# Last forward transform of a four-layer spectral kernel: three result copies moved to VectorE, row products split into row halves

## What is computed

```
def _L3_conv_ref(x, weights):
    x_f = jnp.fft.rfft2(x)
    k_f = jnp.fft.rfft2(weights)
    out_f = jnp.einsum('bchw,ochw->bohw', x_f, k_f)
    return jnp.fft.irfft2(out_f, s=(H, W))
...
x = x + _L0_conv_ref(_gn(x), L0_conv_weights_r, L0_conv_weights_i)
x = x + _L1_conv_ref(_gn(x), L1_conv_gain)
x = x + _L2_conv_ref(_gn(x), L2_conv_weight)
x = x + _L3_conv_ref(_gn(x), L3_conv_weights)
```

## Time and profile before

| | before |
|---|---|
| runs (us) | 966.1, 970.06, 970.32; median 970.06 |
| profiled execution (us) | 970.67 |
| its span (us) | 968.9 |
| busy over the span | TensorE 782.8 (81%), VectorE 599.5 (62%), ScalarE 517.0 (53%), GpSimd 122.5 (13%) |
| granted TensorE clock over the span | 0.928 |
| granted TensorE clock in the last forward stage | 1.00 |
| last forward stage, four groups | 668.70 to 763.17 us of the span |

### The profile page before, as it was taken

The page is one execution under the profiler, slowest core; times in us unless marked ns, Lnnn a source line. Parts: engine busy times, 40 slices in busy tenths (PEclk is TensorE's granted clock), DMA queues, the critical chain, the costliest instruction groups (busy, mean ns, idle before and its releaser), DMA issues. The chain is left out here.

```text
span 968.9 us, 27289 instructions
## 1 busy us (share of the span) xinstructions
PE 782.8 (81%) x10775; PEld 654.1 (68%) x10775; DVE 599.5 (62%) x1112; ACT 517.0 (53%) x868; POOL 122.5 (13%) x120
## 2 busy tenths in 40 slices
PE   5999996853599665787599999984888588879998
PEld 5999995743588543666444444444777488879997
DVE  2555446655856689588777777776666677742222
ACT  0133246743443273465379999004887657765564
POOL 0000000100010044265301222100000100001110
PEclk9999998987789989699799999997999789999999
DMA  7499968532000010000000000004000448831222
GB/s 278 181 342 362 315 206 215 126 87 74 4 1 0 15 26 0 1 1 0 0 2 1 1 1 1 1 1 104 2 0 0 87 88 175 179 81 40 101 107 100
DMA packets 44553, 80.08 MB, mean 83 GB/s; under 512 B 19130, under 2 KB 37568, under 8 KB 40656
## 3 DMA queue, kind: packets, MB, share of 16 engines
q1 hardware_dynamic: 27856, 62.48, 22.7%
q10 hardware_dynamic: 16640, 16.78, 5.1%
HBM read 50.74 MB, written 27.92 MB: 81 GB/s over the span
## 5 line engine op out<-in xcount | busy, mean ns | idle before, releaser
L1462 DVE SCALAR_TENSOR_TENSOR X<-bank,c_power,X 32x512 f32 x128 | 96.8, 756 | 36.5 <-PE bank L1412 32.9
L914 DVE TENSOR_TENSOR X<-X,bank 128x512 f32 x64 | 43.6, 682 | 92.1 <-PE bank L900 92.1
L1605 PE MATMUL bank<-m_xp,m_kf 128*32 128x64 f32 x2048 | 81.7, 246 | 21.7 <-DVE m_xp L1540 10.1
L1605 PEld LDWEIGHTS bank<-m_xp,m_kf 128*32 128x32 f32 x2048 | 80.7, 172 | 22.9 <-issue 22.8
L429 ACT COPY ks_spec<-bank 128x512 f32<-128x512 f32 x64 | 34.3, 589 | 98.6 <-PE bank L357 98.6
L411 DVE COPY ks_rows<-bank 128x512 f32<-128x512 f32 x64 | 41.2, 687 | 70.9 <-PE bank L342 70.9
L215 DVE BATCH_NORM_STATS2 bn<-X 128x6 f32 x128 | 83.1, 683 | 2.9 <-POOL X L1202 1.6
L342 PE MATMUL bank<-ks_fw,ks_src 64*128 64x64 f32 x1024 | 68.7, 298 | 11.2 <-DMA ks_src<-in_L_conv_weights 11.2
L1368 ACT ACTIVATE c_r<-X,c_nrm 32x1024 f32 (+1 forms) x56 | 75.1, 1341 | 2.5 <-DVE c_nrm L1436 1.1
L342 PEld LDWEIGHTS bank<-ks_fw,ks_src 64*128 64x128 f32 x1024 | 68.1, 215 | 11.2 <-issue 11.2
L357 PE MATMUL bank<-ks_fh,ks_rows 64*128 64x128 f32 (+1 forms) x1152 | 71.2, 277 | 0.1
(11 more groups left out here) (186 smaller groups left out, 1869.2 us busy)
## 6 DMA issues: line engine op xcount, KB each, us to landing
ks_src<-in_L_conv_weights SPq DMA_DIRECT2D x8, 2048.0 KB, 8.2
kf<-ks_spec ACTq DMA_DIRECT2D x16, 1024.0 KB, 9.3
m_kf<-kf SPq DMA_DIRECT2D x32, 512.0 KB, 8.5
X<-in_x SPq DMA_DIRECT2D x4, 2048.0 KB, 13.8
out_y<-X SPq DMA_DIRECT2D x16, 512.0 KB, 2.6
xf<-f_xm SPq DMA_DIRECT2D x6, 448.0 KB
l_wb<-in_L_conv_weights_r SPq DMA_DIRECT2D x4, 512.0 KB, 11.0
l_wb<-in_L_conv_weights_i SPq DMA_DIRECT2D x4, 512.0 KB, 13.3
```

The source lines that it names most:

```text
L914: dve.tensor_tensor(x, x, ps[4 + c % 4][:], ALU.add).then_inc(added, 1)
L1462: dve.scalar_tensor_tensor(x, of.rearrange("p (y x) -> p y x", x=HN), filt.power[at, 2:3], x, ALU.mult, ALU.add).then_inc(added, 1)
L1605: last = pe.matmul(ps[4 * half + m // 8][at:at + C, m % 8 * N:(m % 8 + 1) * N], kf[p][:, j, :, H * half + m], xp[half][:, j, m].rearrange( ...
```

## The change

`Forward` gets two more arguments. L0's stage passes `halves` as False and keeps its order. L3's passes True, other tables of normalisation, and `kept_by_dve` = (1, 3, 5).

```
-    def __init__(self, pr, ctx, name, mats, slot_at, rows_by_act, norm_by_act, norm_by_dve):
-        self.pr, self.slot_at = pr, slot_at
+    def __init__(self, pr, ctx, name, mats, slot_at, rows_by_act, norm_by_act, norm_by_dve, halves, kept_by_dve=()):
+        self.pr, self.slot_at, self.halves = pr, slot_at, halves
+        self.keeper = [0 if s in kept_by_dve else 1 for s in range(len(slot_at))]
...
+        self.kept = [pr.sem(f"{name}_kept{e}") for e in range(2)]
...
+    def wait_kept(self, pe, q, first, to):
+        for e in range(2):
+            if e in self.keeper[first:to]:
+                pe.wait_ge(self.kept[e], START + self.keeper.count(e) * q + self.keeper[:to].count(e))
...
+            def half_products(q, j):
+                if j in (0, 2):
+                    self.wait_kept(pe, q - 1, S - 4 + j, S - 2 + j)
+                elif j % 2 == 0:
+                    self.wait_rows(pe, q, j - 3)
+                for k in range(4):
+                    at, col = slice(k * P, (k + 1) * P), (j % 2 * 4 + k) * N
+                    for t, (part, mat) in enumerate(((self.th, 0), (self.th, 1), (self.tl, 0))):
+                        for a in range(2):
+                            half = slice(a * N, (a + 1) * N)
+                            m = pe.matmul(ps[4 + j // 2 % 2 * 2 + a][:, col:col + N], part[j % 4][half, at],
+                                          self.fw[half, mat, half], start=t == 0, stop=t == 2)
+                return m
...
                 pe.wait_ge(self.turned_read, G * q + j + 1)
+                if self.halves:
+                    m = half_products(q, j)
+                    m.then_inc(self.made, 1)
+                    continue
...
     def copy_rows(self, eng, copy, q, j):
+        if self.halves:
+            eng.wait_ge(self.made, self.G * q + j // 2 * 2 + 2)
+            first = j // 2 * 2 * ROWS
+            copy(self.rows[:, first + j % 2:first + 2 * ROWS:2].rearrange("p h r k -> p h (r k)"),
+                 self.pr.psum[4 + j // 2 % 2 * 2 + j % 2][:].rearrange("p (h n) -> p h n", h=ROWS)
+                 ).then_inc(self.rows_read[self.by[j]], 1)
+            return
...
             def keep_filling(s):
-                act.wait_ge(self.made, G * q + NCH + s + 1)
-                keep(q, s).then_inc(self.kept, 1)
+                if self.keeper[s]:
+                    act.wait_ge(self.made, G * q + NCH + s + 1)
+                    keep(q, s).then_inc(self.kept[1], 1)
...
+            def keep_filling(s):
+                if not self.keeper[s]:
+                    dve.wait_ge(self.made, G * q + NCH + s + 1)
+                    keep(q, s).then_inc(self.kept[0], 1)
...
-                if j and not self.by[j - 1]:
-                    self.copy_rows(dve, dve.tensor_copy, q, j - 1)
...
+                behind = 2 if self.halves else 1
+                if j >= behind and not self.by[j - behind]:
+                    self.copy_rows(dve, dve.tensor_copy, q, j - behind)
...
                 normalise_next(NCH + s)
+                if s >= 3:
+                    keep_filling(s - 3)
+            for s in range(S - 3, S):
+                keep_filling(s)
...
-        fwd = Forward(pr, ctx, "f3", mats, SLOT_AT, True, {2: 0, 4: 1, 6: 2, 8: 3}, {9: 4, 10: 5, 12: 6, 14: 7})
+        fwd = Forward(pr, ctx, "f3", mats, SLOT_AT, True, {2: 0, 4: 1}, {3: 2, 8: 3, 9: 4, 11: 5, 13: 6, 14: 7}, True, (1, 3, 5))
```

More of the change, by code:

```diff
@@ L457, in __init__ @@
         self.fw, self.fh, self.fh0 = mats
-        self.turned, self.turned_read, self.high, self.made, self.kept = (
-            pr.sem(f"{name}_{n}") for n in ("turned", "turned_read", "high", "made", "kept"))
+        self.turned, self.turned_read, self.high, self.made = (
+            pr.sem(f"{name}_{n}") for n in ("turned", "turned_read", "high", "made"))
+        self.kept = [pr.sem(f"{name}_kept{e}") for e in range(2)]
         self.ready = [pr.sem(f"{name}_ready{c}") for c in range(NCH)]
@@ L505, in products @@
                 pe.wait_ge(self.turned_read, G * q + j + 1)
+                if self.halves:
+                    m = half_products(q, j)
+                    m.then_inc(self.made, 1)
+                    continue
                 if j < 4:
-                    pe.wait_ge(self.kept, START + S * q + j - 3)
+                    self.wait_kept(pe, q - 1, S - 4 + j, S - 3 + j)
                 else:
@@ L532, in products @@
                 if s >= 4:
-                    pe.wait_ge(self.kept, START + S * q + s - 3)
+                    self.wait_kept(pe, q, s - 4, s - 3)
                 width = self.fh.shape[-1]
@@ L553, in high_parts @@
         pr, ps, S, G = self.pr, self.pr.psum, self.S, self.G
-        act.sem_inc(self.kept, START)
+        for e in range(2):
+            act.sem_inc(self.kept[e], START)
         def group(q, more):
@@ L593, in high_parts, with low_parts @@
         group(Q - 1, False)
-    def low_parts(self, dve):
+    def low_parts(self, dve, keep=None):
         pr, ps, S, G = self.pr, self.pr.psum, self.S, self.G
@@ L614, in group @@
                 normalise_next(j)
-                if j and not self.by[j - 1]:
-                    self.copy_rows(dve, dve.tensor_copy, q, j - 1)
-            if not self.by[NCH - 1]:
-                self.copy_rows(dve, dve.tensor_copy, q, NCH - 1)
+                behind = 2 if self.halves else 1
+                if j >= behind and not self.by[j - behind]:
+                    self.copy_rows(dve, dve.tensor_copy, q, j - behind)
+            for j in range(NCH - behind, NCH):
+                if not self.by[j]:
+                    self.copy_rows(dve, dve.tensor_copy, q, j)
             for s in range(S):
@@ L647, in l0_forward_stage @@
         fwd = Forward(pr, ctx, "f0", mats, [[S * k + s for k in range(4)] for s in range(S)],
-                      False, {1: 0, 3: 1, 5: 2, 7: 3, 9: 4, 11: 5}, {8: 6, 10: 7})
+                      False, {1: 0, 3: 1, 5: 2, 7: 3, 9: 4, 11: 5}, {8: 6, 10: 7}, False)
         xm = pr.sb(ctx, "f0_xm", [P, 2, S, KX, 2, IB])
@@ L715, in _ @@
                     for s in range(S):
-                        pool.wait_ge(fwd.kept, START + S * q + s + 1)
+                        pool.wait_ge(fwd.kept[1], START + S * q + s + 1)
                         pool.tensor_tensor(xm[:, 1, s, :, 0, :], pr.zero[:].unsqueeze(2).broadcast_to([P, KX, IB]),
@@ L1473, in l3_forward_stage, with keep @@
     with ExitStack() as ctx:
-        fwd = Forward(pr, ctx, "f3", mats, SLOT_AT, True, {2: 0, 4: 1, 6: 2, 8: 3}, {9: 4, 10: 5, 12: 6, 14: 7})
+        fwd = Forward(pr, ctx, "f3", mats, SLOT_AT, True, {2: 0, 4: 1}, {3: 2, 8: 3, 9: 4, 11: 5, 13: 6, 14: 7}, True, (1, 3, 5))
+        def keep(copy, q, s):
+            return copy(xm[:, s, :, :, bass.ds(IB * q, IB)].rearrange("p k r b -> p b r k"),
+                        pr.psum[4 + s % 4][:].rearrange("p (b r k) -> p b r k", b=IB, r=2))
         with pr.nc.Block() as block:
@@ L1486, in _ @@
             def _(dve):
-                fwd.low_parts(dve)
+                fwd.low_parts(dve, lambda q, s: keep(dve.tensor_copy, q, s))
             @block.scalar
             def _(act):
-                fwd.high_parts(act, lambda q, s: act.copy(
-                    xm[:, s, :, :, bass.ds(IB * q, IB)].rearrange("p k r b -> p b r k"),
-                    pr.psum[4 + s % 4][:].rearrange("p (b r k) -> p b r k", b=IB, r=2)))
+                fwd.high_parts(act, lambda q, s: keep(act.copy, q, s))
 def load_kernel_spectra(sp, pr, to, i, pair, loaded):
```

## The result

| | before | after |
|---|---|---|
| median of 20 runs (us) | 970.77 (966.1 to 977.34) | 974.78 (969.6 to 977.23) |
| profiled execution, its span (us) | 970.67, 968.9 | 972.49, 970.7 |
| last forward stage in the span | 668.70 to 763.17: 94.47 us | 666.88 to 761.90: 95.02 us |
| mixing, first product to the next stage's first cast of results | 776.68 to 872.43: 95.75 us | 775.40 to 874.22: 98.82 us |
| granted clock over the span | 0.928 | 0.912 |

The ratio of after to before is 1.0032, 95% interval [1.0016, 1.0048]: **slower by 0.32%**, some 3.1 us (the two medians lie 4.0 apart), where 2.6 less was forecast. In the two profiles the forward stage is 0.55 us longer and the mixing 3.07, together 3.6. What lies between them takes 13.5 us in both, what lies behind 96.5.

The account below looks back on a forecast made before the run. An order of waits, not one engine, bounds the last forward stage's groups. Row phases 4 x 0.2, column phases 3 x 0.23 + 1.08: 2.6 us less than 970.06, 967.5 us; range 961.5 to 976.

Parts of the forecast that it names:

- Half products: Row products of 64 rows by 64 columns: one every 0.017 us, 0.40 us per chunk against 0.67.
- rivals 2 and 3: Row products slower than forecast: 0.029 us each, total 974.5, chance 0.22; or 0.055 us each, total 991, chance 0.13.
- rival 2: Row products in halves come no faster than full 64-column ones, 0.029 us: 4.4 us slower, 974.5; chance 0.22.
- The Trainium skill's floor of about 25 ns: Minimum from start to start of TensorE products: 0.60 us per chunk of row products, total 972.3.
- The changes of form: Full-array transposes between half-array row products: 0.15 us idle at each change, up to 1.6 us per group.
- Row phase: Group's first high-part cast to its last row copy: 10.44 us against 10.65, 0.2 less per group, 0.8 for four.
- The walk: Step-by-step dating from a group's first cast: row copy 0 at 3.30, row copy 4 at 7.70, end at 10.44.
- Result copies: Three of eight go from ScalarE to VectorE, taken at 1.09 us each there, a step of 1.0.
- Rival 1: VectorE writes strided results at its contiguous price, 0.69 us: 5.4 us less, 964.7; chance 0.25.
- Column phase: Last row copy to next group's first cast, bound by VectorE: 12.7 against 12.93 us; last group 11.97 against 13.05.
- TensorE's 16 transposes and products hide under both: In the stretch after the row copies, TensorE's work adds no time, in the last group or the others.
- What is saved here is saved at the end: The next stage begins when the last forward stage ends, so its 2.6 us saving reaches the total.

Follow-up runs that it names:

- e10: e8 with 60 instead of 25 added idle products ahead of the mixing loop; 968.45 us, ratio 0.9973 to the kernel before.
- e8: Changed kernel plus 8 idle transposes per group behind the eighth row product and 25 idle products ahead of the mixing loop; 965.35 us, ratio 0.9947.
- e4: Changed kernel plus 13 idle transposes per group behind row products 5, 6 and 7; 970.9 us, ratio 1.0007.
- e5: Kernel before plus 96 idle products ahead of the mixing loop; 969.89 us, ratio 0.9995.
- e3: Kernel before with only the three result copies on VectorE and the new deal of normalisation, row products full; 970.88 us, ratio 0.9994.
- e2: Kernel before with only the row products in halves, result copies and normalisation unchanged; 971.03 us, ratio 1.0006.

## Why the prediction was wrong

- **Half products: right, and a little better than forecast.** 0.015 us each where 0.017 was taken; rivals 2 and 3 fall. That the measured 974.78 lies near rival 2's 974.5 is chance: none of its cause is in the trace. The Trainium skill's floor of about 25 ns (same page, Part 1) doesn't hold for this form either. The changes of form cost the 0.12 to 0.15 us that were taken for them (last half products at 692.66, transposes at 692.78).
- **Row phase: right in direction, undersized.** 0.8 us less a group instead of 0.2. The walk ran late by a little at every hand-over: in the first group the first row copy is at 3.14 instead of 3.30, the third pair's at 7.30 instead of 7.70, and the last ones end at 9.8 and 9.9 instead of 10.44.
- **Result copies: right.** 1.08 us on VectorE where 1.09 was taken (12 copies, 13.0 us). Rival 1's 0.69 falls.
- **Column phase: right in its order of waits, wrong in what it ran at.** At full clock it takes 12.66 (12.7 forecast) and 12.20 in the last group (11.97 forecast). The failed step is "TensorE's 16 transposes and products hide under both": that held only at the granted clock of 1.00 that the rows of before show. Four column phases at the lower clock cost 4 x 1.40 = 5.6 us. Without it the stage would have been, by this estimate, 95.02 - 5.6 = 89.4, or 5.1 less than before (the best run, e10, has 90.16, with its stop in the first group); with it, it is 0.55 more. The prediction counted how much work the row products lose and never asked what TensorE does with the time: in the 2 us ahead of the column phase its busy time went from 1.23 to 0.61.
- **"What is saved here is saved at the end": wrong.** The mixing stage took 3.07 us more: 2.0 because the same products ran slower, at a granted clock of 0.89 instead of 0.94, and 1.0 of idle time, although the stop moved from record 442 to 475 and grew by 1.9, from 1.93 to 3.85 us. e10 against e8 shows that moving the stop back, with an unchanged forward stage, brings 2.4 us of idle time and 3.5 in all. A stop of no known releaser stood in the trace of before, in the stage right behind the changed one and one of 0.70 us in the earlier trace rows, which the prediction used for a rate, and the prediction didn't read that stage at all.
- **A slip in the chances.** Two thirds of 0.25 and a quarter of 0.40 make 0.27, not 0.28; nothing rests on it.

Both were needed for the sign, as far as sums from the profiles tell: with the full clock in the forward stage alone the kernel would come out 2 us ahead (5.1 - 3.1), with the old mixing alone 0.5 behind. The runs nearest to the first case are e4, 0.4 us behind, and e10, 1.7 ahead with an interval that reaches to 1.0001. The prices of single instructions were good; left out was what the rest of the program does to them.

Of the stop, shown is that it has no wait, that instructions added ahead of the loop move it, with places that repeat every 128 records, and change its length. It also goes with instruction packets. Across the 14 profiles TensorE has 101 stops of over 0.4 us without a releaser, and 100 of them end 1.1 to 1.8 us after a 16 KB packet on queue 8 has ended. Most stand in the first layer's mixing, where the kernel before has one every 128 products:

```profile
246.19 2.30 PE L750 MATMUL bank<-l_xb,l_wb 64*32 64x32 f32 x128 [1.42 <-issue]
250.20 2.37 PE L750 MATMUL bank<-l_xb,l_wb 64*32 64x32 f32 x128 [1.72 <-issue]
```

That TensorE waits there for its own code is the reading that fits all of this. That the packet of the long stops is late because it is held up among the loads of kernel spectra is argued from the busy DMA queue beside it; no run took the loads away. Not shown either is why a late stop is cheap in e5 and costly in e10, 31 records earlier, and whether it is the stop that brings the lower clock behind it: in e3 the clock fell behind 1.98 us (0.66 from 795 to 800), in the kernel before it stayed behind 1.93.

## What to carry to other kernels

When an edit makes TensorE faster where TensorE isn't the bound, it only makes it idle: look at what it does in the microseconds ahead of the next stretch that needs it, and fill the gap with products nobody reads if the granted clock falls there. Read the stages behind the changed one for stops with no releaser, since adding instructions moves them, and for their granted clock, since the same products can take 2 us more there. Idle products that are added to move or to fill something act on the clock as well. And compare stages by their own spans, not two executions by their totals, before a saving of a few us is believed or given up.

## What the hardware did that I had not expected

- f16 products of 64 rows by 64 columns on alternating row halves came every 0.015 us, so two of them replace a whole 128-column product (0.056 us) in about half its time.
- The granted clock fell from 2.4 to 1.2 GHz behind 2 us in which TensorE was busy for 0.61, and stayed behind 2 us with 1.23 and with 1.39. In e2 it fell behind 0.84 and stayed behind 0.73.
- TensorE stops without a wait, for 0.4 to 4.2 us in the loop's first pass of the last mixing, and where it does so depends on how many instructions stand ahead of the loop, modulo 128 records: 12 idle products moved it by 24 records in the kernel before. In the first layer's mixing it stops every 128 products, for 0.7 to 1.7 us in the kernel before. Each such stop but one in 101 ends 1.1 to 1.8 us behind a 16 KB packet of instructions.
